# Transposing scaled queries and keys as fp16 halves by DMA instead of by TensorE, with every engine's order rearranged

## The chip, the cores and the metric

The kernel runs on one core of a Trainium2 chip. Its metric is the device time of one launch in microseconds. The core has five engines that run side by side, each through its own list of instructions in order, and wait for each other on semaphores: TensorE (PE: matrix products; PEld is its weight load), VectorE (DVE), ScalarE (ACT), GpSimd (POOL) and SyncE (SP, which here issues the DMAs). TensorE writes to PSUM, eight banks of 2 KB a partition; SBUF is the working memory.

## The reference, cut to what matters

A decoder layer on `x` of 32 batches of 112 tokens by 256, with 375 context rows a batch. Three blocks, each on a layer norm of `x` and each added to it:

```python
# attention, H = 8 heads of D = 128, M = 256
q, k, v = x @ wq, x @ wk, x @ wv           # per head, 112 x 128
q, k = rope(rmsnorm(q)), rope(rmsnorm(k))  # rmsnorm and rotation over the 128
s = (q * mult) @ (k * mult).T              # mult = (1/128) ** 0.5, causal mask
x = x + softmax(s) @ v @ wo
# context
h = layernorm(x) @ ctx.T                   # 112 x 375
x = x + gelu(h) @ ctx
# quantised feed-forward, 256 -> 1024 -> 256
x = x + linear_q(relu_q(linear_q(layernorm(x), w1, b1)), w2, b2)
```

## The kernel before

**Stages.** The loop is a software pipeline over batches, unrolled by four. In turn i each engine works on batch a = i (normalised input, the three projections, rotation and scaling of queries and keys), b = i-1 (scores, softmax, product with the values, output projection), c = i-2 (second layer norm, context block, quantised hidden layer) and, on TensorE and VectorE, d = i-3 (output layer). `FIRST`, `SECOND` and `THIRD` are the turns -1, 0 and 1 with orders of their own. Each engine's `body(i)` is an order written out by hand; every step waits for semaphores that count batches (`done(j)`) or half batches (`half(j, n)`).

**Precision.** Most products are made of three: high times high, high times low, low times high (`split_products`, `project`). A tile in high and low halves is made by a copy to the shorter type on ScalarE and a subtraction on VectorE.

**Queries and keys.** TensorE's `project(w, a, ...)` makes 12 products of 112x512. ScalarE squares the result from PSUM (`square_qk`), VectorE rotates it (`turn_cos`, `turn_sin`, `turn`) and sums the squares a head (`sum_squares`), GpSimd makes the inverse root (`rms_root`). The result is scaled by it into `qkn` (fp32): the queries on ScalarE, eight activations in two groups (`normalise_q`), the keys on VectorE, one instruction (`normalise_k`, L510). In the next turn TensorE transposes sixteen blocks of 112x128 into PSUM (`transpose_qk`, L888), ScalarE copies them to fp16 (`qkT_hi`) and VectorE subtracts to get `qkT_lo` (L557). Then come the scores.

**PSUM.** Banks are shared, so a writer must wait for the last reader of what lay there. The one that the argument turns on:

```python
q_ps, k_ps, v_ps = psum[0:T, 4:6, :], psum[0:T, 2:4, :], psum[0:T, 0:2, :]   # L194
f_ps = psum[:, 4:6, 0:FC // 2 * T]                                           # L203
pe.wait_ge(f_int_done, half(a.plus(-3), 1))                                  # L996, before project(0, a)
```

`f_ps` is the hidden layer of batch c, which ScalarE's `hidden(c)` reads at the end of its turn (eight activations, L788); `q_ps` is where the next turn's query projection goes.

**DMAs.** SP stores the output rows of d, loads the context of batch c+2 twice (rows, 375 KB, once ScalarE and GpSimd have split the last; columns, 375 KB, once they are used) and `x` of batch b+4 once its slot is free.

## Time and profile before

| | us |
|---|---|
| median of 3 runs (lowest to highest) | 731.12 (730.54 to 731.15) |
| the profiled execution | 730.84 |
| its span, first to last instruction | 728.8 |
| TensorE busy in it | 694.8 (95%) |
| VectorE busy | 654.9 (90%) |
| ScalarE busy | 518.7 (71%) |
| GpSimd busy | 308.5 (42%) |
| hardware DMA queue, share of 16 engines | 17.5% |

The profile is of one execution. Busy times are unions of an engine's instructions; an instruction's own duration is longer than the step to the next queued one, as neighbours overlap. The granted clock of TensorE was full in all but the first and the last slices of the page (0.985 over the span).

### The profile page before, as it was taken

The page shows a single profiled execution, that of the slowest core. Times are in us where ns is not written, and L with a number is a line of the kernel's source. Part 1 is how long each engine was busy: PE and PEld are TensorE (multiplying, and loading weights), DVE is VectorE, ACT ScalarE, POOL GpSimd, SP SyncE. Part 2 cuts the span into 40 slices and gives each one's busy share as a digit, 9 for nine tenths or more (in the row PEclk, how much of TensorE's full clock was granted, in tenths as well). Part 3 has the DMA queues.
Part 4 walks back from the last instruction along what each step waited for, and adds up shares of the span by engine and source line. Part 5 has one row for each costly group of instructions (what it writes and reads, how often), then busy time and mean ns, then how long its engine had stood idle before and what let it go on. Part 6 is the DMA issues. An engine that isn't in the chain of part 4 may idle for free.

```text
span 728.8 us, 15471 instructions
## 1 busy us (share of the span) xinstructions
PE 694.8 (95%) x5600; PEld 611.3 (84%) x5600; DVE 654.9 (90%) x1264; ACT 518.7 (71%) x1290; POOL 308.5 (42%) x425
## 2 busy tenths in 40 slices
PE   5599999999999999999999999999999999999974
PEld 4478888898888989898898989889888988988863
DVE  5989999999999999999999999999999999999942
ACT  5657666777766677776667877666777766777742
POOL 1344434534444443444444344444434444543421
PEclk9799999999999999999999999999999999999996
DMA  7601111011111101111110111111011111101100
GB/s 255 217 7 49 51 57 53 25 49 49 48 55 55 51 22 49 48 48 55 55 47 24 51 48 48 55 55 46 23 52 49 48 55 56 48 18 48 44 7 13
DMA packets 23946, 38.86 MB, mean 53 GB/s; under 512 B 2048, under 2 KB 18896, under 8 KB 23664
## 3 DMA queue, kind: packets, MB, share of 16 engines
q1 hardware_dynamic: 23920, 38.51, 17.5%
q8 instruction: 16, 0.26, 0.2%
q14 instruction: 10, 0.08, 0.0%
HBM read 34.84 MB, written 3.67 MB: 53 GB/s over the span
## 4 chain that ended last, share of the span: by engine, by line
PE 87%; DVE 5%; ACT 3%; issue 2%; DMA 1%; POOL 1%; SPq 0%; POOLq 0%; DVEq 0%; ACTq 0%
PE psum L880 34%; PE psum L867 22%; PE psum L908 7%; PE psum L888 7%; PE psum L945 5%; PE psum L978 4%; PE psum L970 3%; PE psum L915 3%; PE psum L936 2%; DMA w_raw<-in_wv 1%; DVE turn_c L489 1%; DVE ss L481 1%; DVE turn_s L498 1%; POOL rms L357 1%; ACT w_raw L764 1%
## 5 line engine op out<-in xcount | busy, mean ns | idle before, releaser
L880 PE MATMUL psum<-wqkv_hi,xnT_hi 128*112 128x512 f32 x384 | 159.7, 416 | 4.8 <-DVE wqkv_lo L446 2.7
L880 PE MATMUL psum<-wqkv_lo,xnT_hi 128*112 128x512 f32 x384 | 152.5, 397 | 0.0
L880 PE MATMUL psum<-wqkv_hi,xnT_lo 128*112 128x512 f32 x384 | 131.8, 397 | 0.0
L350 POOL TENSOR_TENSOR rstd<-ve,nhalf 112x1 f32<-112x1 f32 x96 | 55.5, 578 | 142.7 <-DVE ve L420 137.7
L357 POOL TENSOR_TENSOR rms<-ms,nhalf 112x8 f32<-112x8 f32 x64 | 106.3, 1662 | 5.0
L718 ACT ACTIVATE sq<-psum 112x1024 f32<-112x1024 f32 x64 | 65.0, 1015 | 59.4 <-PE psum L880 59.4
L764 ACT ACTIVATE w_raw<-psum,rden 112x128 f32<-112x128 f32 x256 | 69.6, 384 | 45.4 <-DVE rden L532 45.4
L361 POOL TENSOR_TENSOR ctx_lo<-ctx_in,ctx_hi 125x768 fp32r<-125x768 f32 x32 | 58.6, 1830 | 92.5 <-ACT ctx_hi L691 92.5
L880 PEld LDWEIGHTS psum<-wqkv_hi,xnT_lo 128*112 128x112 f32 x384 | 67.7, 176 | 22.3
L880 PEld LDWEIGHTS psum<-wqkv_hi,xnT_hi 128*112 128x112 f32 x384 | 68.1, 177 | 20.4 <-issue 3.1
L774 ACT ACTIVATE qkn<-turn_c,rms 112x128 f32<-112x128 f32 x256 | 83.1, 427 | 1.1 <-POOL rms L357 1.1
L481 DVE TENSOR_REDUCE ss<-sq 112x4 f32<-112x512 f32 (+1 forms) x95 | 81.9, 862 | 0.0
L880 PEld LDWEIGHTS psum<-wqkv_lo,xnT_hi 128*112 128x112 f32 x384 | 68.3, 178 | 15.0
L489 DVE TENSOR_TENSOR turn_c<-psum,cos_t 112x1024 f32<-112x1024 f32 x64 | 77.9, 1217 | 1.4 <-ACT sq L718 1.4
L867 PE MATMUL psum<-wo_hi,oT_hi 128*112 128x256 f32 x256 | 78.2, 306 | 0.7 <-DVE oT_lo L564 0.7
L505 DVE TENSOR_TENSOR turn_c<-turn_c,turn_s 112x1024 f32<-112x1024 f32 x64 | 77.9, 1217 | 0.1
L498 DVE TENSOR_TENSOR turn_s<-psum,sin_t 112x1024 f32<-112x1024 f32 x64 | 77.4, 1210 | 0.0
L867 PE MATMUL psum<-wo_hi,oT_lo 128*112 128x256 f32 x256 | 71.8, 280 | 0.0
L867 PE MATMUL psum<-wo_lo,oT_hi 128*112 128x256 f32 x256 | 71.5, 279 | 0.0
L557 DVE TENSOR_TENSOR qkT_lo<-psum,qkT_hi 128x896 f16<-128x896 f32 x64 | 69.4, 1086 | 0.1
L788 ACT ACTIVATE f_int<-psum,b_col 128x112 int16<-128x112 f32 x256 | 66.6, 399 | 1.8 <-PE psum L970 1.8
L908 PEld LDWEIGHTS psum<-v_sb,w_raw 112*112 112x112 f32 x512 | 60.8, 176 | 3.6
(90 smaller groups left out, 1725.9 us busy)
## 6 DMA issues: line engine op xcount, KB each, us to landing
ctx_in<-in_ctx_rows SPq DMA_DIRECT2D x32, 375.0 KB
ctxT<-in_ctx_cols SPq DMA_DIRECT2D x32, 375.0 KB, 6.4
x_in<-in_x SPq DMA_DIRECT2D x32, 112.0 KB, 2.0
out_y<-y_out SPq DMA_DIRECT2D x32, 112.0 KB, 1.9
w_raw<-in_w SPq DMA_DIRECT2D x2, 1024.0 KB, 6.5
w_raw<-in_wq SPq DMA_DIRECT2D x2, 512.0 KB, 4.6
w_raw<-in_wk SPq DMA_DIRECT2D x2, 512.0 KB, 6.6
w_raw<-in_wv SPq DMA_DIRECT2D x2, 512.0 KB, 8.5
```

The source lines that it names most:

```text
L357: pool.tensor_tensor(rms[:, w, :], ms[:, w, :], nhalf[:, 0:H], ALU.pow).then_inc(qk_rms_done[w], 1)
L481: return dve.tensor_reduce(ss[:, w, hs], heads(sq[:, w, :])[:, hs, :], AX_X, ALU.add)
L489: dve.tensor_tensor(turn_c[:, w, :].rearrange("t (b h d) -> t b h d", b=2, d=D), (q_ps, k_ps)[w].rearrange("t b (h d) -> t b h d", d=D), c ...
L498: dve.tensor_tensor(turn_s[:, w, :].rearrange("t (h two f) -> t h two f", two=2, f=HALF), halves, table, ALU.mult).then_inc(sin_done[w], 1)
L505: dve.tensor_tensor(turn_c[:, w, :], turn_c[:, w, :], turn_s[:, w, :], ALU.add).then_inc(qk_turned[w], 1)
L557: dve.tensor_tensor(qkT_lo[:, w, :].rearrange("p (b n) -> p b n", b=2), (qT_ps, kT_ps)[w], qkT_hi[:, w, :].rearrange("p (b n) -> p b n", b=2),
L764: last = act.activation(on[:, h * D:(h + 1) * D], o_ps[:, h // OH, (h % OH) * VW:(h % OH) * VW + D], ACT.Copy, scale=rden[:, h:h + 1])
L774: last = act.activation(qkn[:, 0, h * D:(h + 1) * D], turn_c[:, 0, h * D:(h + 1) * D], ACT.Copy, scale=rms[:, 0, h:h + 1])
L788: last = act.activation(f_int[:, c * T:(c + 1) * T], f_ps[:, c // (FC // 2), (c % (FC // 2)) * T:(c % (FC // 2) + 1) * T], ACT.Relu, bias= ...
L867: product = pe.matmul(dst, lh, rh, start=first and k == 0, stop=last and k == len(terms) - 1)
L880: last = pe.matmul(ps[:, n, :], left[:, c, :], right[:, c, w, n * BANK:(n + 1) * BANK], start=c == 0 and left is xnT_hi and right is wqkv_ ...
L908: last = pe.matmul(o_ps[:, h // OH, at:at + VW], p_sb[:, h * T:(h + 1) * T], v_sb[:, h, :], start=h % OH == 0, stop=h % OH == OH - 1 or h ...
```

## The change

Queries and keys are now treated alike. ScalarE scales the rotated rows into fp16 (`normalise_qk`, eight activations each), VectorE subtracts that from the scaled row in eight instructions each (`split_qk`), and both halves lie in token layout in `qk16`. SP then issues one DMA transpose each for queries and keys, 112 x 2048 fp16 (448 KB) from SBUF to SBUF, straight into the layout of the scores. TensorE's transposes and the copies and subtractions after them go. The output layer's PSUM tile moves from bank 7 to bank 3. SP's loop is written out for all batches instead of looping. The orders of the engines are rearranged; the diff has them all.

```diff
+        qk16 = sb("qk16", [T, 2, 2, HD], F16)
+        qkT = sb("qkT", [P, 2, 2 * H, T], F16)
-        f2_ps = bank(7, M)[0:T]
+        f2_ps = bank(3, M)[0:T]
...
 SP
+            def transpose_qk(w, j):
+                sp.wait_ge(qk_lo_done[w], done(j))
+                sp.dma_start_transpose(qkT[:, w], qk16[:, w].rearrange("t l n -> t (l n)")).then_inc(
+                    qkT_landed[w][j.off % SLOTS], 16)
...
                     load_ctxT(nxt)
                 nxt = b.plus(SLOTS)
+                if a.inside(B):
+                    if b.inside(B):
+                        sp.wait_ge(s_ready, done(b))
+                    transpose_qk(0, a)
+                    transpose_qk(1, a)
                 if b.inside(B) and nxt.inside(B):
                     sp.wait_ge(x2_done, done(b))
                     load_x(nxt)
-            iterations(sp, body)
+            for n in range(-1, B + 3):
+                body(Batch(0, n))
...
 GpSimd
                 if C:
                     split_ctx(c)
+                if A:
+                    rms_root(0, a)
                 if B_ and A:
                     mask_later_keys(b)
-                if A:
-                    rms_root(0, a)
...
 VectorE
+            def split_qk(w, j):
+                dve.wait_ge(qk_hi_done[w], done(j))
+                for h in range(H):
+                    at = slice(h * D, (h + 1) * D)
+                    last = dve.scalar_tensor_tensor(out=qk16[:, w, 1, at], in0=turn_c[:, w, at], scalar=rms[:, w, h:h + 1],
+                                                    in1=qk16[:, w, 0, at], op0=ALU.mult, op1=ALU.subtract)
+                last.then_inc(qk_lo_done[w], 1)
...
 ScalarE
-            def normalise_q(n, j):
+            def normalise_qk(w, n, j):
                 if n == 0:
-                    act.wait_ge(q_turned, done(j))
-                    act.wait_ge(q_rms_done, done(j))
+                    act.wait_ge(qk_turned[w], done(j))
+                    act.wait_ge(qk_rms_done[w], done(j))
+                    if j.has(1):
+                        act.wait_ge(qkT_landed[w][(j.off - 1) % SLOTS], landed(j.plus(-1)))
                 for h in range(n * HH, (n + 1) * HH):
-                    last = act.activation(qkn[:, 0, h * D:(h + 1) * D], turn_c[:, 0, h * D:(h + 1) * D],
-                                          ACT.Copy, scale=rms[:, 0, h:h + 1])
+                    last = act.activation(qk16[:, w, 0, h * D:(h + 1) * D], turn_c[:, w, h * D:(h + 1) * D],
+                                          ACT.Copy, scale=rms[:, w, h:h + 1])
                 if n == 1:
-                    last.then_inc(q_normed, 1)
+                    last.then_inc(qk_hi_done[w], 1)
```

The orders of one steady turn, before and after (a, b, c, d as above; n is the batch after a):

```
TensorE before: transpose_qk(0), (1) b | project q a | out_units d | xn2 rows c | scores b | ctx_hidden c
                project k a | weigh_values b | ctx_out c | project v first half a | transpose_o(0) b
                project v second half a | transpose_o(1) b | xn1 rows n | project_out b, 4 heads, with
                transpose_xq c after two | hidden_units c | project_out b, last 4 heads
TensorE after:  project q a | out_units d | xn2 rows c | ctx_hidden c | project k a | scores b | ctx_out c
                project v first half a | weigh_values b | project v second half a | transpose_o(0), (1) b
                then as before
VectorE before: split_qkT(0) b | normalise_x2 c | split_qkT(1) b | residual_out d | turn_cos, turn_sin(0) a
                sum_squares(0) a | gelu_inner c | normalise_x n | gelu_outer c | turn(0) a | split_g c
                turn_cos(1) a | invert_sums b | turn_sin(1) a | residual_ctx c | sum_squares(1) half a
                split_oT(0) b | quantise_x3 c | sum_squares(1) half a | split_oT(1) b | turn(1) a
                split_xnT n | normalise_k a | residual_attention b | stats | clip_hidden c
VectorE after:  normalise_x2 c | residual_out d | turn_cos, turn_sin(0) a | gelu_inner c | sum_squares(0) a
                gelu_outer c | turn(0) a | split_g c | normalise_x n | turn_cos, turn_sin(1) a
                residual_ctx c | sum_squares(1) a | invert_sums b | split_qk(0) a | quantise_x3 c
                split_oT(0) b | turn(1) a | split_oT(1) b | split_xnT n | split_qk(1) a
                residual_attention b | stats | clip_hidden c
ScalarE before: split_qkT(0), (1) b | square_qk(0) a | copy_xn2T, split_ctx c | softmax_exp b
                square_h, tanh_h, split_g c | square_qk(1) a | normalise_o(0), (1) b | split_oT(0) b
                copy_v(0), normalise_q(0) a | split_oT(1) b | split_xnT n | copy_xqT c
                copy_v(1), normalise_q(1) a | hidden c
ScalarE after:  split_ctx c | square_qk(0) a | copy_xn2T, square_h, tanh_h, split_g c | square_qk(1) a
                softmax_exp b | normalise_qk(0), both groups a | normalise_o(0), (1) b | copy_v(0) a
                split_oT(0) b | copy_v(1) a | split_oT(1) b | split_xnT n | copy_xqT c
                normalise_qk(1), both groups a | hidden c
```

## Rows read from the trace of the kernel before

**Rows 1.** The page, first section: busy time, share of the span, instructions.
```profile
PE 694.8 (95%) x5600; PEld 611.3 (84%) x5600; DVE 654.9 (90%) x1264; ACT 518.7 (71%) x1290; POOL 308.5 (42%) x425
```

**Rows 2.** Windows, one steady turn: length, busy of each engine, clock, DMA.
```profile
326.20:347.50 21.30, 21.30 (x177) 18.88 (x176) 20.03 (x40) 15.78 (x42) 9.58 (x13) 1.00 0.16 47
```

**Rows 3.** Chain of waits, one steady turn: start us, us, what.
```profile
304.88 1.68 PE psum L888 x16
306.56 2.80 PE psum L880 x12
...
315.78 1.77 PE psum L908 x16
```

**Rows 4.** Chain of waits, batch 2's projection and the tail.
```profile
50.99 2.81 PE psum L880 x12
...
668.70 2.80 PE psum L880 x12
...
692.45 1.42 PE psum L867 x24
...
700.02 2.17 ACT w_raw L764 x8
```

**Rows 5.** Timeline of ScalarE, same turn: start us, us, instruction, idle before it.
```profile
337.25 1.01 ACT L718 ACTIVATE sq<-psum 112x1024 f32<-112x1024 f32 x1
339.70 2.17 ACT L764 ACTIVATE w_raw<-psum,rden 112x128 f32<-112x128 f32 x8 [1.45 <-DVE rden L532]
341.76 0.55 ACT L691 ACTIVATE oT_hi<-psum 128x448 fp32r<-128x448 f32 x1
...
345.29 1.27 ACT L774 ACTIVATE qkn<-turn_c,rms 112x128 f32<-112x128 f32 x4
346.46 2.05 ACT L788 ACTIVATE f_int<-psum,b_col 128x112 int16<-128x112 f32 x8
```

**Rows 6.** Groups by line and shape: busy us, mean ns, idle before.
```profile
L557 DVE TENSOR_TENSOR qkT_lo<-psum,qkT_hi 128x896 f16<-128x896 f32 x64 | 69.4, 1086 | 0.1
```

**Rows 7.** Timeline of VectorE, same turn.
```profile
331.55 0.42 DVE L584 SCALAR_TENSOR_TENSOR y_out<-psum,x3b 112x256 f32<-112x256 f32 x1 [0.67 <-PE psum L978]
331.89 1.21 DVE L489 TENSOR_TENSOR turn_c<-psum,cos_t 112x1024 f32<-112x1024 f32 x1
...
336.32 0.50 DVE L522 SCALAR_TENSOR_TENSOR g<-h_t,psum 125x336 f32<-125x336 f32 x1 [0.23 <-ACT h_t L738]
...
339.43 0.23 DVE L532 RECIPROCAL rden<-psum 112x6 f32<-112x6 f32 x2
...
342.50 0.61 DVE L564 TENSOR_TENSOR oT_lo<-psum,oT_hi 128x448 fp32r<-128x448 f32 x1
343.03 0.41 DVE L550 TENSOR_SCALAR xq_int<-x,mv,rstd 112x256 int16<-112x256 f32 x1
...
343.61 0.68 DVE L481 TENSOR_REDUCE ss<-sq 112x4 f32<-112x512 f32 x1
344.42 0.63 DVE L564 TENSOR_TENSOR oT_lo<-psum,oT_hi 128x448 fp32r<-128x448 f32 x1
344.96 1.21 DVE L505 TENSOR_TENSOR turn_c<-turn_c,turn_s 112x1024 f32<-112x1024 f32 x1
...
346.40 1.68 DVE L510 TENSOR_TENSOR qkn<-turn_c,rms 112x1024 f32<-112x1024 f32 x1
```

**Rows 8.** Timeline of TensorE, a projection that starts after a stall.
```profile
21.61 0.49 PE L880 MATMUL psum<-wqkv_hi,xnT_hi 128*112 128x512 f32 x1 [2.04 <-DVE xnT_lo L439]
...
24.03 0.63 PE L880 MATMUL psum<-wqkv_hi,xnT_lo 128*112 128x512 f32 x2
```

**Rows 9.** DMA issues: tile, queue, count, KB each, median us to landing.
```profile
ctxT<-in_ctx_cols SPq DMA_DIRECT2D x32, 375.0 KB, 6.4
x_in<-in_x SPq DMA_DIRECT2D x32, 112.0 KB, 2.0
```

**Rows 10.** Windows in the tail.
```profile
690.00:695.00 5.00, 2.70 (x34) 2.27 (x34) 2.95 (x6) 2.02 (x4) 0.97 (x3) 1.00 0.08 23
```

More of the change, by code:

```diff
@@ L672, in body @@
                 if A:
-                    normalise_k(a)
+                    split_qk(1, a)
                 if B_:
@@ L850, in body @@
                 if A:
-                    copy_v(1, a)
-                    normalise_q(1, a)
+                    normalise_qk(1, 0, a)
+                    normalise_qk(1, 1, a)
                 if C:
@@ L883, in project, with scores @@
                     last.then_inc(ready, 1)
[L885 to L886 removed]
+            def scores(j):
+                pe.wait_ge(qT_landed[j.off % SLOTS], landed(j))
+                pe.wait_ge(kT_landed[j.off % SLOTS], landed(j))
                 for h in range(H):
[L888 to L897 removed]
                     last = split_products(s_ps[:, h // HH, (h % HH) * T:(h % HH + 1) * T],
[L899 removed]
+                                          [((qkT[:, 1, h, :], qkT[:, 1, H + h, :]), (qkT[:, 0, h, :], qkT[:, 0, H + h, :]))])
                 last.then_inc(s_ready, 1)
@@ L997, in body @@
                     project(0, a, q_ps, q_ready)
-                if i is THIRD:
-                    pe.wait_ge(v_copied, half(b, 1))
-                    transpose_qk(0, b)
-                    pe.wait_ge(k_sin_done, done(b))
-                    transpose_qk(1, b)
                 if D_:
                     out_units(d)
-                if B_ and not A:
-                    scores(b)
                 if C:
@@ L1010, in body @@
                     transpose_rows(xn2T_ps, xn2, xn2T_ready)
-                if B_ and A:
-                    scores(b)
-                if C:
-                    if c.has(1):
-                        pe.wait_ge(out_done, done(c.plus(-1)))
                     ctx_hidden(c)
+                if D_:
+                    pe.wait_ge(out_done, done(d))
+                if i is THIRD:
+                    pe.wait_ge(k_sin_done, done(b))
                 if A:
@@ L1019, in body @@
                 if B_:
-                    if A:
-                        pe.wait_ge(q_sin_done, done(a))
-                    weigh_values(b)
+                    pe.wait_ge(v_copied, half(b, 1))
+                    scores(b)
                 if C:
```

131 lines of the change are left out of this document (50 added, 81 removed).

## The prediction

> **What bounds the kernel now.** I read the page's first section first: TensorE is busy 95% of the span, VectorE 90% [rows 1], so either may be the bound. A window over one steady turn of the loop settles it: of 21.30 us TensorE is busy all, VectorE 20.03, ScalarE 15.78, GpSimd 9.58 [rows 2]. The chain of waits there consists of TensorE alone, block behind block: the sixteen transposes of queries and keys take 1.68 us of it, a whole projection 2.80, the value product 1.77 [rows 3]. In that chain the query projection of batch 2 starts at 50.99 and that of batch 31 at 668.70 [rows 4]: 29 turns of 21.30 us, with 51.0 us ahead of them and 60.1 behind.
>
> So 1.68 us of TensorE's work goes, which leaves 19.6 a turn. Whether that is gained depends on who is next. ScalarE's eight hidden-layer activations start at 346.46 and take 2.05, so they end at 348.51 [rows 5]. The transposes of 304.88 come round at 347.5 and end at 349.2 (two turns after [rows 3]), and then the next query projection runs, which overwrites the PSUM banks that the activations read (the wait on f_int_done in TensorE's body). The transposes cover 1.0 us of that wait; the slack behind it is some 0.6. If only the transposes went, TensorE would stand still for 1.0 of the 1.68 us. So that wait is what I follow in the new order.
>
> **The change part by part.**
>
> *TensorE*: minus 1.68 us a turn [rows 3]; everything else is moved, nothing added.
>
> *VectorE* loses two subtractions of 896 columns (1.086 each [rows 6], 1.00 start to start) and the key scaling (1.68, 1.61 start to start). It gains sixteen scalar_tensor_tensor of 112x128, which the trace doesn't show. Its queued ops step by their length at 0.96 elements a ns plus 0.065: 448 elements took 0.53 (342.50 to 343.03) [rows 7]. So 128 take 0.20 and sixteen 3.2. Ends: 0.17 if half the fixed part goes, 0.29 if nothing overlaps (the 0.42 of a 256-wide op at 331.55 less 128 elements). I take 0.20, as every queued row overlaps its neighbour. VectorE goes from 20.0 to 19.6 us, between 19.1 and 21.0.
> The Trainium skill ("VectorE: DVE Perf Modes", Side-by-side: where the cycles go) puts some 158 cycles ahead of an instruction's elements. By that a half costs 0.30 us, sixteen 4.8, and VectorE has 21.1 us a turn. The rows speak against it for queued instructions: the 448-wide one would step by 0.63, and it steps by 0.53.
>
> *ScalarE* loses two copies (0.86 each start to start, an estimate: 896 columns against 448 in 0.44) and gains eight key scalings, of which four take 1.17 (345.29 to 346.46) [rows 5]: 2.34. It goes to 16.4 us. The sum is no danger; the place is. The key scalings stand directly ahead of the hidden-layer activations, and wait for turn(1), which VectorE does after split_oT(0).
>
> *The loop this closes.* I walked all queues in their new order with start-to-start steps from these rows and 0.04 us for a semaphore. The same walk of the old order gives 21.32 us a turn, with waits of VectorE of 0.8 us before residual_out (0.67 at 331.55) and 0.3 before gelu_outer (0.23 at 336.32) [rows 7]. The new order, from the start of a query projection:
> - A projection that starts after a stall takes 3.0 us to its end (21.61 to 24.66 [rows 8]), 0.2 more than one behind other work. out_units 0.87, then residual_out 0.34 on VectorE: turn_cos(0) starts at 4.3; ScalarE's squares (1.01 [rows 5]) are done by then.
> - From turn_cos(0) to turn(1) VectorE took 344.96 - 331.89 = 13.07 us [rows 7]. Out go the idle 0.23 before gelu_outer, the second split_oT (0.54) and the 0.21 idle before it (343.61 + 0.60 to 344.42), and 0.07 for one reduction in place of two: 12.0. In comes split_qk(0), 1.6: 13.6. The last of it are invert_sums (0.15 start to start), split_qk(0), quantise_x3 (0.58) and split_oT(0) (0.53).
> - invert_sums so ends at 15.2. ScalarE scales the heads (2.06, 339.70 to 341.76), copies half of the values (0.48) and makes oT_hi (0.55) [rows 5]: 18.4. VectorE is at split_oT(0) at 17.3 and waits 1.1 for it.
> - split_oT(0) 0.53, turn(1) 1.21: 20.2. Key scalings 2.34, hidden-layer activations 2.05, semaphores: 24.6. Only then may the next query projection start.
>
> Unrounded the walk gives 24.32 and with the 0.2 of the restart 24.55, which I take. TensorE has 19.6 us of work and stands still for 4.7.
>
> *The landing*: split_qk(1) ends 24.3 us after the turn's start, and the scores are due 8.7 into the next turn. So each transfer may take 8.7 us from SP's queue to landing, hidden by the query projection, out_units, ctx_hidden and the key projection. A transfer of 448 KB within SBUF is in no row. Nearest: 112 KB landed in 2.0 us and 375 KB in 6.4, at whose rate 448 KB take 7.6 [rows 9]. Ends 2 and, if it moves in small pieces at half that rate, 15. I take 4 to 8, hidden. SP's new waits (scores, low halves; both behind the context loads) hold back the load of x, three batches ahead, and the next store, whose buffer is wanted four turns on: nothing.
> The Trainium skill ("DMA: Bandwidth & Descriptors", Latency and other measured facts) has 261 GB/s for a DMA transpose with a strided middle dimension. By that 458,752 bytes move in 1.8 us and the first rival below drops out. No trace here shows a transpose by DMA.
>
> *GpSimd*: same instructions; the mask now follows the queries' root, and still ends before the value product is due. Nothing.
>
> *Head and tail.* At the head ScalarE does eight key scalings (2.34) where it copied the transposed keys (0.97), ahead of the output weights, which VectorE awaits: plus 1.4, so 52.4. At the tail the last scores began 23.75 us after the last query projection (692.45 - 668.70) [rows 4]; now 24.3 + 0.4 + 4, plus 5.0. Against that the context product no longer runs behind them: the heads were scaled at 700.02 [rows 4], 7.6 after the scores began, and without it some 5.3 (scores, exponential, mask, value product). Net plus 2.7: 62.8.
>
> **Sum.** 52.4 + 29 x 24.55 (712.0) + 62.8 = 827.2 us of span. The profiled execution took 730.84 for a span of 728.8, so 2.0 lie around it: 829. It is 0.3 under the median of the runs shown, 731.12, which is nothing here.
>
> **Rivals.**
> 1. *The keys land late.* If a transfer takes L over 8.7 us, the loop is the landing, then scores to value product (5.5), invert_sums to oT_hi (3.3), split_oT(0), turn(1), scalings (4.2), split_qk(1) 1.6 and some 0.4 of semaphores and issue: L + 15. At L = 12 it is 27 a turn, 900 us; at 15, 987. For it: 7.6 us by the context's rate. Against it: nothing leaves the chip, and little else moves then.
> 2. *The halves are dear on VectorE.* Up to 0.33 each they hide in the 1.1 us wait. At 0.4 the walk gives 25.4 a turn, 853 us; at 0.5, 27.0, 900. Against it: no 256-wide row is over 0.43.
> 3. *Faster: TensorE stays the bound.* The one mechanism: the loop over f_int_done is shorter than TensorE's own 19.6 us, which then decides, and the run takes 731 - 30 x 1.68 = 681. Up to 21.3 the loop would still leave a gain. For it: VectorE and ScalarE each have less work than TensorE. Against it: with every stall left out the loop's rows still sum to 3.0 + 1.1 + 13.6 + 1.2 + 2.34 + 2.05 + 0.1 = 23.4. I would have to be 2 us off on a path of measured steps.
> 4. *TensorE's clock falls in the gaps.* In the tail it was granted 1.00 with TensorE busy 2.70 of 5 us [rows 10]; here it would be busy 19.6 of 24.5. At the lower of its two levels throughout, TensorE alone would need 39 us a turn, some 1,250 in all.
>
> **How the numbers follow.** Forecast 69%: 829, its own range 795 (23.4 a turn, no stall at split_oT) to 858 (25.5, if VectorE's new steps beside GpSimd stretch as the key scaling did: 1.68 where an addition of that length took 1.21 [rows 7]). Late landing 13%, dear halves 5%, clock 4%, faster 7%, and 2% for a loop that ends at the old time. A measurement of this kernel can tell about 0.2% from no change. Slower 0.91, same 0.02, faster 0.07. The range 788 to 875 leaves out the faster case, the clock and most late landings.
>
> **What would show it.** Right: in a steady turn TensorE idles 4 to 5 us, the largest piece (1.7) right before the query projection, the others before transpose_o and project_out; ScalarE goes from key scalings into the activations without a gap; VectorE waits about 1.1 us for oT_hi and 1.7 for the keys' high halves. Wrong: scores released by a DMA (rival 1), a mean of the halves over 0.33 (rival 2), TensorE without gaps (rival 3), a granted clock under 1 in the steady part (rival 4), or a turn under 23.4 us.

## The result and the profile after

| | before | after |
|---|---|---|
| median us (lowest to highest, runs) | 730.83 (730.49 to 731.15, 4) | 869.21 (868.35 to 874.89, 4) |
| profiled execution, span | 730.84, 728.8 | 869.32, 867.4 |
| mean granted clock of TensorE | 0.985 | 0.946 |

The changed kernel takes 1.1906 times as long (95% interval 1.1874 to 1.1938). It was forecast slower, at 829; it is 40 us slower than that. It lies inside the range of 788 to 875, but above 858, where the prediction had the upper end for its own mechanism: that the range holds it is in part luck.

The page's first section, to be read against [rows 1]. TensorE lost its 512 transposes but not its busy time, since a matmul counts longer where the engine restarts or runs at half clock (one of 512 columns 0.48 and 0.63 us, queued at full clock 0.40); VectorE got 38 us more.

```profile
PE 716.8 (83%) x5088; PEld 585.0 (67%) x5088; DVE 693.2 (80%) x1649; ACT 548.7 (63%) x1482; POOL 361.8 (42%) x425
```

Windows of 25 us, about one turn each, with the columns of [rows 2]. No engine is full now. TensorE stands still for 3.65 us of the first window, less than the 4 to 5 that the prediction gave as its sign. In the second its clock is under 1.

```profile
322.00:347.00 25.00, 21.35 (x161) 17.44 (x160) 21.24 (x52) 16.71 (x46) 11.39 (x15) 1.00 0.34 77
347.00:372.00 25.00, 21.28 (x150) 16.98 (x148) 19.58 (x50) 15.86 (x46) 9.73 (x13) 0.93 0.33 73
```

The chain of waits over one steady turn, from query projection to query projection: 25.02 us (forecast 24.55). In [rows 3] it was TensorE alone. Now it goes from TensorE to VectorE (314.62 to 325.6), to ScalarE (heads, 325.63), through `split_oT` (328.76) and the output projection (329.44) to `copy_xqT` (330.55), the key scalings (L775), the hidden layer's activations (L789), and back: the loop that the prediction walked, save for the two steps at 329.44 and 330.55.

```profile
310.21 3.05 PE psum L881 x12
313.26 0.89 PE psum L971 x8
...
314.62 1.22 DVE turn_c L501
...
325.63 0.06 ACT w_raw L763
...
328.30 0.44 ACT oT_hi L695
...
328.76 0.64 DVE oT_lo L573
...
329.44 0.96 PE psum L868 x6
...
330.55 0.04 ACT xqT L695
...
333.24 1.95 ACT f_int L789 x8
...
335.23 3.04 PE psum L881 x12
```

The view of waits (who waited for whom: us in total, times, longest). The first two are the new standstills of VectorE and TensorE. The last is the only one of TensorE for a transfer of queries or keys, and it is in the head.

```profile
DVE qk L524 <- ACT qk L775: 64.2, 32, 2.7
PE psum L881 <- ACT f_int L789: 42.7, 29, 1.8
...
PE psum L868 <- DMA qkT<-qk: 7.4, 1, 7.4
```

The timeline of VectorE in that turn, against [rows 7]. The eight halves at 325.51 are followed 2.09 us later, so they step by 0.26; `xq` takes 0.64; and VectorE reaches `split_oT` at 328.7, just when oT_hi is there.

```profile
325.51 2.17 DVE L524 SCALAR_TENSOR_TENSOR qk<-turn_c,rms,qk 112x128 f16<-112x128 f32 x8
327.60 0.41 DVE L565 TENSOR_SCALAR xq_int<-x,mv,rstd 112x256 int16<-112x256 f32 x1
328.04 0.64 DVE L418 TENSOR_SCALAR xq<-xq_int 112x256 bf16<-112x256 int16 x1
328.76 0.62 DVE L573 TENSOR_TENSOR oT_lo<-psum,oT_hi 128x448 fp32r<-128x448 f32 x1
```

The DMA issues, against [rows 9]: a transpose of 448 KB lands 4.0 us after its issue. The context's columns land in 5.8 us (6.4 before), `x_in` in 2.9 (2.0).

```profile
qkT<-qk SPq DMA_TRANSPOSE x64, 4.0
```

TensorE's timeline (first two lines) and a 5-us window. After a standstill of 1.82 us the query projection begins with matmuls that step by 0.23 to 0.30 us, as everywhere; from 361.0 on they step by 0.43. The granted clock of the window is 0.66: TensorE runs at the lower of its two levels (1.2 instead of 2.4 GHz) for 3.4 us, then is back.

```profile
360.27 0.46 PE L881 MATMUL psum<-wqkv_hi,xnT_hi 128*112 128x512 f32 x1 [1.82 <-ACT f_int L789]
...
363.12 0.63 PE L881 MATMUL psum<-wqkv_hi,xnT_hi 128*112 128x512 f32 x1
```
```profile
360.00:365.00 5.00, 4.73 (x16) 3.50 (x16) 2.46 (x12) 0.98 (x3) 3.07 (x5) 0.66 0.58 115
```

In such windows from 90 to 785 us there are 37 us at half clock in all, eleven stretches; a turn with one takes 25.3 to 26.6 us. The kernel before has none from 90 to 660.

**Where the 40 us are.** The landmark is the square of a batch's queries on ScalarE, which starts as their projection ends: batch 2's at 59.19, batch 3's at 85.86, batch 31's at 794.41. The forecast puts 3.0 us between a projection's start and its square.

| part | forecast | measured | more |
|---|---|---|---|
| start to square of batch 2 | 52.4 + 3.0 = 55.4 | 59.2 | 3.8 |
| 29 turns | 712.0 | 794.41 - 59.19 = 735.2 | 23.2 |
| square of batch 31 to the end | 62.8 - 3.0 = 59.8 | 867.4 - 794.41 = 73.0 | 13.2 |

The tail's chain, against [rows 4]. The exponential (L727) stands behind `split_g` on ScalarE, GpSimd's mask (L385) behind the exponential, GpSimd's low half of the context (L373) behind the mask, and the context product (828.55) behind that; the value product (L901) is queued behind it on TensorE. The heads are scaled (L763) at 833.57, which is 42.2 us after the last query projection began (794.41 - 3.0); before it was 31.3, the forecast says 34.0. The value product takes 2.48 us here and 1.93 in a batch before; the granted clock is 0.72 from 820 to 840 and 0.63 from 840 to 867, where [rows 10] showed 1.00. From the heads to the end it is 33.8 us (867.4 - 833.57), and before it was 28.8 (728.8 - 700.02): 5.0 more, of which some 3.5 are steps that run through TensorE's matmuls at half clock, and 1.5 a scaling on VectorE that takes 1.88 us beside GpSimd (see the last section). So 8.2 of the 13.2 us that the forecast missed lie ahead of the heads and 5.0 behind them.

```profile
824.64 0.81 ACT w_raw L727
...
825.71 0.93 POOL w_raw L385
826.64 1.78 POOL ctx_lo L373
...
828.55 2.23 PE psum L868 x9
830.79 2.48 PE psum L901 x16
...
833.57 2.18 ACT w_raw L763 x8
```

### The profile page after: what moved, and what is told of

It reads as the page before. It is cut to its first block, busy times and chain, and to the rows that moved or that the text cites. A ratio compares the mean times of both kernels' runs of the same rounds, so it can differ in the third digit from the quotient of the medians.

```text
span 867.4 us, 14896 instructions
## 1 busy us (share of the span) xinstructions
PE 716.8 (83%) x5088; PEld 585.0 (67%) x5088; DVE 693.2 (80%) x1649; ACT 548.7 (63%) x1482; POOL 361.8 (42%) x425
## 2 busy tenths in 40 slices
DMA packets 140684, 68.23 MB, mean 79 GB/s; under 512 B 118784, under 2 KB 135632, under 8 KB 140400
## 3 DMA queue, kind: packets, MB, share of 16 engines
q1 hardware_dynamic: 140656, 67.88, 33.8%
## 4 chain that ended last, share of the span: by engine, by line
DVE 42%; ACT 26%; PE 21%; issue 8%; DMA 1%; POOL 1%; SPq 1%; ACTq 0%; POOLq 0%; DVEq 0%
PE psum L881 11%; ACT qk L775 8%; DVE turn_c L501 8%; DVE turn_s L510 8%; ACT w_raw L763 7%; ACT f_int L789 6%; DVE ss L493 6%; PE psum L868 5%; DVE turn_c L517 4%; PE psum L971 3%; DVE oT_lo L573 2%; ACT v_sb L695 2%; DVE h_t L531 2%; DVE g L537 2%; DVE stat L423 2%
## 5 line engine op out<-in xcount | busy, mean ns | idle before, releaser
L881 PE MATMUL psum<-wqkv_hi,xnT_hi 128*112 128x512 f32 x384 | 162.7, 424 | 49.0 <-ACT f_int L789 42.7
L524 DVE SCALAR_TENSOR_TENSOR qk<-turn_c,rms,qk 112x128 f16<-112x128 f32 x512 | 139.7, 346 | 64.2 <-ACT qk L775 64.2
L775 ACT ACTIVATE qk<-turn_c,rms 112x128 f16<-112x128 f32 x512 | 156.4, 389 | 27.2 <-POOL rms L369 25.9
L369 POOL TENSOR_TENSOR rms<-ms,nhalf 112x8 f32<-112x8 f32 x64 | 150.6, 2353 | 5.0
L360 POOL TENSOR_TENSOR ve<-mv,ln_eps 112x1 f32<-112x1 f32 x64 | 14.6, 228 | 298.7 <-DVE mv L428 298.7
L868 PE MATMUL psum<-wo_hi,oT_hi 128*112 128x256 f32 x256 | 83.9, 328 | 21.3 <-DVE oT_lo L573 21.2
L763 ACT ACTIVATE w_raw<-psum,rden 112x128 f32<-112x128 f32 x256 | 69.7, 384 | 44.0 <-DVE rden L547 44.0
L510 DVE TENSOR_TENSOR turn_s<-psum,sin_t 112x1024 f32<-112x1024 f32 x64 | 77.8, 1216 | 0.0
L493 DVE TENSOR_REDUCE ss<-sq 112x8 f32<-112x1024 f32 x64 | 77.5, 1210 | 0.0
L868 PE MATMUL psum<-wo_hi,oT_lo 128*112 128x256 f32 x256 | 76.4, 298 | 0.0
L868 PE MATMUL psum<-wo_lo,oT_hi 128*112 128x256 f32 x256 | 76.1, 297 | 0.0
L367 POOL TENSOR_TENSOR ms<-ss,rms_eps 112x8 f32<-112x8 f32 x64 | 18.5, 288 | 129.1 <-DVE ss L493 129.1
L901 PEld LDWEIGHTS psum<-v_sb,w_raw 112*112 112x112 f32 x512 | 60.8, 182 | 14.4 <-issue 14.4
```

The costliest lines, as they stand in the source:

```text
L369: pool.tensor_tensor(rms[:, w, :], ms[:, w, :], nhalf[:, 0:H], ALU.pow).then_inc(qk_rms_done[w], 1)
L493: return dve.tensor_reduce(ss[:, w, hs], heads(sq[:, w, :])[:, hs, :], AX_X, ALU.add)
L510: dve.tensor_tensor(turn_s[:, w, :].rearrange("t (h two f) -> t h two f", two=2, f=HALF), halves, table, ALU.mult).then_inc(sin_done[w], 1)
L524: last = dve.scalar_tensor_tensor(out=qk16[:, w, 1, at], in0=turn_c[:, w, at], scalar=rms[:, w, h:h + 1], in1=qk16[:, w, 0, at], op0=ALU.m ...
L763: last = act.activation(on[:, h * D:(h + 1) * D], o_ps[:, h // OH, (h % OH) * VW:(h % OH) * VW + D], ACT.Copy, scale=rden[:, h:h + 1])
L775: last = act.activation(qk16[:, w, 0, h * D:(h + 1) * D], turn_c[:, w, h * D:(h + 1) * D], ACT.Copy, scale=rms[:, w, h:h + 1])
```

## Experiments

All are variants of the changed kernel, unless said otherwise. Each median stands beside the kernel before on the same chip (731.37, 730.26, 730.43 and 731.26 in the four sets).

### Is the bank shared with the hidden layer what holds the query projection?

`e1_banks` puts the hidden layer's sums into banks 2 and 3, so that the key projection waits for its activations in place of the query projection.

```diff
-        f_ps = psum[:, 4:6, 0:FC // 2 * T]
+        f_ps = psum[:, 2:4, 0:FC // 2 * T]
@@ body of TensorE
-                        pe.wait_ge(f_int_done, half(a.plus(-3), 1))
                     project(0, a, q_ps, q_ready)
...
+                        pe.wait_ge(f_int_done, half(a.plus(-3), 1))
                     project(1, a, k_ps, k_ready)
@@ hidden_units and out_units wait for all readers of those banks
+                        pe.wait_ge(oT_lo_done, half(b, 1))
-                    if c % (FC // 2) == 0:
-                        pe.wait_ge(f_q_done, half(j, c // (FC // 2)))
+                pe.wait_ge(f_q_done, half(j, 1))
```

> The hidden layer's PSUM tile moves from banks 4 and 5 to banks 2 and 3, so that the query projection no longer waits for f_int; the wait stands before the key projection instead. Theory A (the loop from the key scalings over the hidden-layer activations to the query projection sets the turn): the query projection starts as soon as TensorE is there, and the same path comes back 0.8 us shorter a turn over out_units, which waits for the clipped hidden layer: some 24.2 us a turn against 25.0, about 845 us in all. Rival B (the keys' landing sets the turn) and rival C (VectorE's sixteen small instructions set it): the wait was slack, the time stays at 869.

Measured 846.78 us (845.89 to 847.67), ratio 1.1581 [1.1539, 1.1624]; an undisturbed turn is 24.2 us, and three stretches at half clock are left of eleven. The size came as expected, which is in part luck: the mean turn fell by 1.03 us (25.31 to 24.28), as stretches at half clock went too, and head and tail together are some 5 us longer here. The wait is real, and 0.8 us a turn lie behind it, not more: the next loop is close. It runs through the same key scalings, but on through VectorE. The chain of that kernel from them to the next `copy_xn2T`:

```profile
325.07 0.99 ACT qk L775 x3
326.08 0.36 DVE qk L524 x2
...
326.61 1.66 DVE qk L524 x6
...
329.80 0.28 DVE f_q L580
...
330.12 1.08 PE psum L970 x8
```

### Does the place of the key scalings matter?

`e9_hidfirst` turns the two around on ScalarE: first the activations, then the keys.

```diff
 @@ body of ScalarE
-                if A:
-                    normalise_qk(1, 0, a)
-                    normalise_qk(1, 1, a)
                 if C:
...
                     hidden(c)
+                if A:
+                    normalise_qk(1, 0, a)
+                    normalise_qk(1, 1, a)
```

> ScalarE's hidden-layer activations go ahead of the key scalings. If only the wait at the query projection counts, f_int is ready 2.4 us earlier and the turn falls to about 23.3 us, 820 in all. Theory A in full says that it gets worse: the key scalings end 2 us later, VectorE stands in split_qk(1) until then, and the clipping of the hidden layer, which is VectorE's last step, comes later, so that out_units right behind the query projection waits some 3 us for it. By the walk of the queues the turn is 2.0 us longer than now: 27.0, about 927 us.

Measured 988.19 us (987.01 to 989.37), ratio 1.3515 [1.3463, 1.3568]; turns of 28.2 to 29.5 us. Slower, as the walk of the queues says, and worse than it says. The wait that was avoided (query projection on `f_int`) is down to 0.5 us, and VectorE's for the keys' high halves is up to 5.1 (in the changed kernel 2.7):

```profile
DVE qk L524 <- ACT qk L775: 145.5, 32, 5.1
```

The miss of 61 us is in part the clock: 160 us of 810 are at half clock, one or two stretches in every turn. A change that looked like freeing TensorE lengthens the loop, since behind the keys on VectorE stand the statistics and `clip_hidden`, for which `out_units` waits.

### Was the stall at `split_oT` a term of its own?

`e3_copy` lets ScalarE make oT_hi before it copies half of the values (0.48 us earlier).

```diff
 @@ body of ScalarE
-                if A:
-                    copy_v(0, a)
                 if B_:
                     split_oT(0, b)
                 if A:
+                    copy_v(0, a)
                     copy_v(1, a)
```

> ScalarE copies the first half of the values after split_oT(0) instead of before it. Theory A: oT_hi is ready 0.48 us earlier, which VectorE waits for before turn(1), and all of it comes off the turn: 24.55 against 25.0, about 855 us. Rivals B and C: no change, 869.

Measured 865.01 us (863.18 to 866.83), ratio 1.1831 [1.1763, 1.1898]; an undisturbed turn is 24.85. Of the 0.48 us, 0.15 come through. oT_hi is there at 530.93 in the turn looked at, but VectorE gets to `split_oT` only at 531.34, busy with its halves (2.2 us) and with `quantise_x3` (0.82 and 0.23 in this turn). The 1.1 us of stall that the forecast had there were no stall but VectorE's work.

### Are the halves dear, or the bound?

`e2_whole` makes the low halves by one subtraction of 1024 columns. It leaves the root mean square out of the low halves.

```diff
-                for h in range(H):
-                    at = slice(h * D, (h + 1) * D)
-                    last = dve.scalar_tensor_tensor(out=qk16[:, w, 1, at], in0=turn_c[:, w, at], scalar=rms[:, w, h:h + 1],
-                                                    in1=qk16[:, w, 0, at], op0=ALU.mult, op1=ALU.subtract)
+                last = dve.tensor_tensor(qk16[:, w, 1, :], turn_c[:, w, :], qk16[:, w, 0, :], ALU.subtract)
```

> VectorE makes each low half with one subtraction over 1024 columns instead of eight scalar_tensor_tensor; the scale by the root is left out of the low halves, and only of them. VectorE has 2.0 us less work a turn. Theory A: before split_oT(0) VectorE only waits longer for oT_hi, and the second split is off the path, so the turn stays at 25.0, about 869 us, at most 0.2 us a turn less. Rival C (VectorE's small instructions set the turn): 2.0 us a turn less, about 811 us.

Measured 869.29 us (866.86 to 871.73), ratio 1.1889 [1.1804, 1.1974]; undisturbed turns as in the changed kernel. VectorE has 74 us less to do in all (busy 619.4), one instruction of 1.21 us in place of eight in 2.2, and the time stays. What it wins before `split_oT` it loses there, waiting for oT_hi (1.46 us in this line of its timeline):

```profile
327.37 0.62 DVE L570 TENSOR_TENSOR oT_lo<-psum,oT_hi 128x448 fp32r<-128x448 f32 x1 [1.46 <-ACT oT_hi L692]
```

So rival 2 is out: the halves cost a third more than I took, and it costs nothing. With `e3_copy` this shows the two paths into `split_oT(0)`, ScalarE's and VectorE's, to be within 0.15 us of each other; shortening one alone brings no more than that.

### Do the transfers hold anything?

`e4_extra1` puts one spare transpose of half the size ahead of the keys' and waits for it; `e5_extra3` three in a row.

```diff
                 sp.wait_ge(qk_lo_done[w], done(j))
+                if w == 1:
+                    sp.wait_ge(spare_set, 1)
+                    for n in range(1):   # 3 in e5_extra3
+                        sp.dma_start_transpose(spare[:, :, :], spare_in[:, :]).then_inc(spare_landed, 16)
+                        sp.wait_ge(spare_landed, 16 * (1 * (done(j) - 1) + n + 1))   # 3 * (done(j) - 1) in e5_extra3
                 sp.dma_start_transpose(qkT...
```

> SP transposes a spare tile of half the size by DMA and waits for its landing before it issues the keys' transpose, so that the keys land some 3 us later than now (7 us after the low halves are done, against 4.0). Theory A: the keys have 8.7 us, nothing changes, 869. Rival B (the landing is on the path): 3 us a turn more, about 956.

Measured 868.43 us (866.59 to 870.27), ratio 1.1887 [1.1846, 1.1929].

> The same with three spare transposes in a chain, so that the keys land some 9 us later, 13 us after the low halves. Now the slack of 8.7 is used up and the loop over the landing, L + 15, sets the turn: 28 us, about 956 in all. If the slack were much larger than I worked out, the time would stay at 869.

Measured 1011.11 us (1009.62 to 1012.59), ratio 1.384 [1.3799, 1.3882]. The DMA table and the waits of the latter:

```profile
spare<-spare_in SPq DMA_TRANSPOSE x96, 2.7
```
```profile
PE psum L877 <- DMA qkT<-qk: 118.0, 32, 15.7
```

One spare transfer, 2.7 us to landing, is hidden whole; three show, 3.3 us of wait a turn behind the head's 15.7. So in the changed kernel the keys have at least 2.7 us to spare, and rival 1 is a real mechanism that lies beyond this kernel's transfers. Its size here is 55 us over what was expected: turns of 26.7 to 32 us, mean 29.6, with 118 us at half clock.

### What would it bring to leave the transposes out, with nothing put in their place?

`e6_notr` is the kernel before with four of its sixteen transposes a batch. It leaves the other heads' blocks of transposed queries and keys unwritten (zeros at first).

```diff
                 pe.wait_ge(qk_normed[w], done(j))
-                for h in range(H):
+                for h in range(0, H, HH):
```

> The kernel before, with two of eight transposes of queries and of keys each; the other heads' blocks are left out of the computation (PSUM is zeroed once at the start). TensorE has 1.2 us less work a turn. If TensorE alone set the turn, the time would fall by 30 x 1.2, to 695. By the slack that I read (0.6 us before the query projection meets f_int) most of it is lost to that wait: the walk gives 20.9 us a turn against 21.3, about 719.

Measured 721.83 us (720.86 to 724.42), ratio 0.9893 [0.9866, 0.9919]; a turn is 20.95 us against 21.30. Twelve transposes of 0.105 us (a sixteenth of 1.68 [rows 3]) are 1.26 us, and 0.35 come through. The prediction said that most of it would be lost in the wait on f_int_done. The size is right, the culprit is another one: that wait is 0.3 us long, and the chain comes from VectorE's key scaling (L510), which the few transposes that are left wait for:

```profile
321.07 1.69 DVE qkn L510
...
322.81 0.41 PE psum L889 x2
```

The kernel before is balanced in this sense: these twelve transposes are worth less than a third of their length to it, some 1%, and any new step on the other engines has to be paid for out of that. What it would bring to have none left that waits for the key scaling was not run.

### How much of the loss is the new order, and how much the halves and the DMA?

`e7_oldorder` has the DMA transposes and the halves, with the engines' orders of the kernel before: on VectorE both `split_qk` follow `turn(1)`, where the key scaling was; on ScalarE the key scalings follow the query scalings; GpSimd masks ahead of the queries' root; TensorE's body as before, without the transposes. The diff is against the kernel before.

```diff
 @@ body of VectorE, at the place of normalise_k
-                    normalise_k(a)
+                    split_qk(0, a)
+                    split_qk(1, a)
 @@ body of ScalarE
-                    normalise_q(1, a)
+                    normalise_qk(0, 1, a)
+                    normalise_qk(1, 0, a)
+                    normalise_qk(1, 1, a)
```

> The change's DMA transposes with the order of every engine as before it; split_qk(0) and split_qk(1) stand where normalise_k stood, the key scalings behind those of the queries, ahead of the hidden layer. If the new order is what the change needs to be worth anything, this is slower than 869. By the walk of the queues it is 1.1 us a turn faster than the new order: split_oT(0) no longer waits, and the loop is the same otherwise; 23.9 us a turn, about 837. In either case it is slower than before (731), as the loop over the key scalings and the hidden-layer activations is there too.

Measured 859.95 us (859.7 to 860.19), ratio 1.1771 [1.1742, 1.1801]. The old order is 1.1% faster than the new one, and slower than expected by 23 us. A steady turn takes 25.24 in the mean, and every one has one or two stretches at half clock, 130 us of 695. TensorE stands still for 3.4 us before the query projection, and this is what it then does (chain of that kernel):

```profile
306.89 1.94 ACT f_int L790 x8
...
308.87 5.46 PE psum L882 x12
314.33 1.27 PE psum L972 x8
```

At full clock these two took 3.04 and 0.89. So some 2.8 us of this turn's 26.1 are the clock's, and without them it is 23.3: near the expected 23.9 (this turn alone; an estimate). The loss is thus in what the change does, halves on the scaling path ahead of the activations, in either order. The 9 us that the old order is faster do not come from the steady turns, whose means are 25.24 and 25.31, but from the tail: from the square of batch 31 to the end it takes 64.1 us (858.0 - 793.87) where the changed kernel takes 73.0.

### Do the standstills bring the half clock?

`e8_fill` puts five idle matmuls of 512 columns ahead of the wait on f_int_done; `e12_fillall` seven there, three ahead of the transposes of the heads and three ahead of the output projection. No result of theirs is read.

```diff
                     if a.has(3):
+                        for _ in range(7):   # e8_fill: 5, with xnT_hi[:, 0, :] in place of the first wqkv_hi
+                            pe.matmul(psum[0:T, 7, :], wqkv_hi[:, 0, 0, 0:T], wqkv_hi[:, 0, 0, 0:BANK], start=True, stop=True)
                         pe.wait_ge(f_int_done, half(a.plus(-3), 1))
 @@ e12_fillall also ahead of transpose_o(0, b) and of project_out(range(0, HH // 2), b)
+                        for _ in range(3):
+                            pe.matmul(psum[0:T, 3, :], wqkv_hi[:, 0, 0, 0:T], wqkv_hi[:, 0, 0, 0:BANK], start=True, stop=True)
...
```

> The changed kernel with five matmuls of 512 columns into an unused bank right before TensorE waits for f_int; their result is used by nobody. They take 1.2 of the 1.7 us that TensorE stands still there. If the dips of TensorE's clock that the trace shows (stretches of 3.4 us at 0.5 in about every third turn) come from its standing still, they go, and with them the 0.3 us a turn by which the mean turn (25.3) exceeds the undisturbed one (25.0); the restart of the query projection saves up to 0.2 more: 24.8 a turn, about 855 us. If the dips have another cause, or cost nothing, the time stays at 869.

Measured 865.49 us (862.0 to 867.16), ratio 1.1834 [1.179, 1.1877]; 20 us at half clock in the steady part, where the changed kernel had 37. Fewer, not gone: 0.57 us of standstill were left ahead of the query projection, and the other two pauses were whole. Six stretches against eleven alone would say little: `e4_extra1` and `e11_tail`, with the pauses of the changed kernel, have nine each, `e2_whole` has thirteen.

> Thirteen idle matmuls of 512 columns a turn (into banks that are free there, results never read) stand in TensorE's pauses: seven ahead of the wait for the hidden layer's activations, three ahead of the transposes of the heads, three ahead of the output projection. Theory: the stretches at half clock come from TensorE's pauses, and go if all are filled: of the eleven in the steady part none is left, the granted clock there is 1.00, turns stay at 25.0 us, and the run takes some 859 us (29 turns times 0.35 less). Rival: they come from the power of the other engines or from TensorE's load itself: at least as many as before (eleven), 869 us or more.

Measured 862.63 us (860.08 to 863.43), ratio 1.1782 [1.1755, 1.1808]. A window of it: TensorE is busy 24.16 of 25 us, at 1.00.

```profile
322.00:347.00 25.00, 24.16 (x173) 19.55 (x174) 21.29 (x52) 16.70 (x47) 11.07 (x13) 1.00 0.34 77
```

No 5-us window from 90 to 785 us is under 1.00, all turns lie between 24.93 and 25.04, and their mean is 24.96 against 25.31. More work for TensorE, less time: the dips came from its pauses, and cost 0.35 us a turn. The run is 6.6 us faster than the changed kernel's median; I had expected 10. In the profiles the 28 turns give the 9.8 us, and head and tail are 4 us longer here (batch 3's square at 87.39 against 85.86, the tail 75.4 against 73.0).

### The tail

`e11_tail` lets GpSimd make the low half of the context ahead of the mask in the drain as well.

```diff
 @@ body of GpSimd
-                if B_ and not A:
-                    mask_later_keys(b)
                 if C:
                     split_ctx(c)
                 if A:
                     rms_root(0, a)
-                if B_ and A:
+                if B_:
                     mask_later_keys(b)
```

> GpSimd forms the low half of the context ahead of the mask in the drain too, as it does in a steady turn. Theory: the tail's excess hangs in part on GpSimd's order: the mask waits for the exponential at 825.5 and ctx_lo (1.8 us) behind it releases the context product at 828.55, ahead of which the value product can't run. With ctx_lo early, the context product starts when the low half of g is there (about 825.2) and the value product at about 827.3 in place of 830.8: 3.5 us less, 865.7 us. Rival: the exponential, behind split_g on ScalarE, sets it, and under 1 us is gained: 869 us.

Measured 868.14 us (867.55 to 870.78), ratio 1.1877 [1.1852, 1.1902], which doesn't tell it from the changed kernel. In its profile the tail (square of batch 31's queries to the end) is 865.9 - 794.99 = 70.9 us instead of 73.0, and the value product follows the mask directly:

```profile
819.78 1.89 DVE xn L485
...
828.25 0.81 ACT w_raw L725
...
829.31 0.94 POOL w_raw L385
...
830.30 2.04 PE psum L899 x16
```

From the end of the mask to the end of the value product it is 2.1 us instead of 6.6, but the mask ends 3.0 us later after that square. Of these, 1.3 are the context's hidden product, which ran at half clock (2.87 us, in the changed kernel 1.58), and 1.5 the edit's own doing: the low half of the context (GpSimd, 819.71 to 821.5) now runs beside VectorE's scaling L485, which takes 1.89 us instead of 0.42. So the wait for ctx_lo was real, and moving it up costs part of what it gives. The 2.1 us in all are within the spread of tails: `e8_fill` and `e12_fillall`, whose drain is the changed kernel's, have 73.1 and 75.4. The rest of the excess is read from the chain: the exponential behind the GELU steps on ScalarE, and the clock.

### The best that these parts give

`e10_halves` joins `e1_banks` and `e3_copy`, and ScalarE signals each group of four high halves, so that VectorE starts on the first four.

```diff
-                if n == 1:
-                    last.then_inc(qk_hi_done[w], 1)
+                last.then_inc(qk_hi_done[w], 1)
 @@ split_qk
-                dve.wait_ge(qk_hi_done[w], done(j))
                 for h in range(H):
+                    if h % HH == 0:
+                        dve.wait_ge(qk_hi_done[w], half(j, h // HH))
```

> Three repairs together: the hidden layer's tile in banks 2 and 3 (846 us alone), the first copy of the values behind split_oT(0) (865 alone), and ScalarE signals each group of four scaled heads, so that VectorE starts with the low halves 1.2 us earlier. Theory A: what is left of the loop runs over split_qk(1) and the clipping to out_units, and the halves take 1.1 us out of it: 22.7 us a turn by the walk of the queues, about 795. If VectorE's own work (20.6 us a turn with halves of 0.263 start to start) and not the chain of waits held the turn, little would come of it beyond the 24.2 of the banks alone.

Measured 808.09 us (806.2 to 813.06), ratio 1.1075 [1.1024, 1.1126]; undisturbed turns of 23.05 us, two stretches at half clock. 44% of the loss is back, and it is still 10.7% slower than the kernel before. VectorE's wait for high halves fell from 64.2 to 23.9 us. I expected 22.7 a turn and 795.

## Why the prediction was right, and where it was short

**Right: the direction and the loop.** The next query projection waits for the activations behind the key scalings, and these for what stands behind `split_oT(0)`. Landmarks from the projection's start, forecast and measured (310.21 onwards): `turn_cos(0)` 4.3 and 4.4; end of `invert_sums` 15.2 and 15.4; oT_hi 18.4 and 18.5; the wait of TensorE before the projection 1.7 and up to 1.8; that of VectorE for the high halves 1.7 and 1.9 to 2.0. `e1_banks` cut the loop where it was said to close, and the turn fell; `e9_hidfirst` closed it worse.

**Right: no transfer shows in a steady turn.** 4.0 us to landing, in the forecast's 4 to 8. `e4_extra1` showed at least 2.7 us of room, `e5_extra3` that the room has an end.
The Trainium skill's 261 GB/s ("DMA: Bandwidth & Descriptors", Latency and other measured facts) would make it 1.8 us, an estimate; from issue to landing this case measured more than twice that, with some 1.5 us of it SP's issue. By the skill's figure and by the trace alike, rival 1 drops out here.

**Mis-sized: the halves, 0.20 us.** They step by 0.26 (2.09 for eight; 346 ns mean in the group of 512), inside the bounds of 0.17 and 0.29. The choice by a plain tensor_tensor's fixed part was too low for one with a scalar pointer and three sources, but it cost nothing: `e2_whole`.
The Trainium skill ("VectorE: DVE Perf Modes", Side-by-side: where the cycles go) gives 0.30 for it, an estimate from its fixed cycles: 0.04 above the measured step, where my 0.20 is 0.06 below.

**Mis-sized: the stall of 1.1 us at `split_oT(0)`.** It is about 0.1. VectorE arrives at 18.5 where the walk had 17.3: 0.2 in the first part, 0.5 by the halves, 0.4 by `xq` (0.64 us beside GpSimd's addition, 0.24 in the tail).

**Mis-sized: the turn, 24.55.** It is 24.96 without dips. The step that failed is the last third of the walk. It had `turn(1)` release the key scalings; `copy_xqT` stands before them on ScalarE and waits for TensorE, which has to restart the output projection first (329.44 to 330.55). The scalings start at 330.80, some 0.25 us after `turn(1)` would have let them, and the first part of the walk took 0.1 to 0.15 more; scalings and activations took their 4.4. Over 29 turns the 0.4 us are 11.7. (A slip in the sum itself, 24.32 and 0.2 taken as 24.55, is 0.9 us in all.)

**Given as a rival, and it came in part: the clock.** "TensorE's clock falls in the gaps" stood at 4%, for a fall throughout. It fell in eleven stretches of 3.4 us. `e12_fillall` priced it: 28 turns times 0.35, 9.8 us. A granted clock under 1 in the steady part was a sign of being wrong by the prediction's own list. The step that failed is the reading of [rows 10]: a window in which TensorE is busy 2.70 of 5 us at 1.00 doesn't show that a steady loop with pauses of 1.8 us stays at 1.00. Another window of the kernel before, in its head, pointed the other way:

```profile
30.00:35.00 5.00, 2.00 (x19) 1.68 (x19) 4.21 (x11) 2.84 (x3) 0.89 (x2) 0.50 0.12 37
```

The third part of the turns' 23.2 us is 1.7, batch 2's own turn (26.67).

**Mis-sized: the head, plus 1.4.** It is 5.4 more than before (square of batch 2: 51.0 + 2.8 and 59.2). Three steps of it show in the trace. First, the scores of batch 0 wait for their transfer, with nothing beside them to hide it; they start at 35.39, before it was 33.54, though the last weights landed 1.3 us earlier in this run. The chain of the head:

```profile
26.20 2.11 DVE qk L524 x8
28.33 2.82 SPq L312
31.20 4.05 DMA qkT<-qk
```

I walked ScalarE in the head and left out the landing, though the prediction counted it (with 4 us) for the tail.

Second, GpSimd: the prediction put its new order at nothing, since the mask, behind the queries' root, "still ends before the value product is due". In the head it does not. The exponential ends at 38.81 and TensorE is through with half of the values' projection at 41.8, but the mask runs only at 44.01, behind the root and a small step of its own (L354) that takes 1.98 us here, beside VectorE's work, and 0.18 in a steady turn:

```profile
40.42 1.69 POOL L369 TENSOR_TENSOR rms<-ms,nhalf 112x8 f32<-112x8 f32 x1
42.07 1.98 POOL L354 TENSOR_TENSOR pool_cell<-pool_cell 1x1 f32<-1x1 f32 x1
44.01 0.98 POOL L385 TENSOR_SCALAR_AFFINE_SELECT w_raw<-w_raw 112x896 f32<-112x896 f32 x1
```
```profile
45.09 3.75 PE L901 MATMUL psum<-v_sb,w_raw 112*112 112x129 f32 x16 [3.33 <-issue]
```

That is 3.3 us of standstill before the value product. The kernel before had the mask ahead of the root, at 37.17, and no such pause; nor has `e7_oldorder`, with that order, and its square of batch 2 is at 55.50.

Third, the clock: the value product takes 3.75 us there and 1.93 before; the half clock lasts from 30.0 to 50.4, in the kernel before from 27.2 to 37.4. Together the three make the scaled heads 7.1 us late (49.16 against 42.04), and 1.7 of that are won back before batch 2's projection, where TensorE no longer has transposes.

In a steady turn the mask ends at 323.12 and the value product begins at 323.22, so there too GpSimd is only just in time.

**Mis-sized most, for its length: the tail, plus 2.7.** It is 15.7 more than before (from the square of batch 31: 728.8 - 668.70 - 2.80 = 57.3, and 73.0). The forecast counted that the context product no longer ran behind the last scores, and missed that its low half does stand between mask and value product (GpSimd's order in the drain), that the exponential is behind the GELU steps on ScalarE, and the clock. What it did count, 4 us for the landing, is not what held the scores: the keys' transfer was issued at 817.1 and landed some 4.0 later, and the scores began at 821.89, right behind the context's hidden product in TensorE's order. `e7_oldorder` shows the new order to be the larger part: with the old one the tail is 64.1, so some 9 of the 15.7 us hang on it (one profile each). `e11_tail` shows that the wait for ctx_lo is one step of that; how the rest divides between the exponential's place and the clock is read from the chain and not tested.

**Rivals 2 and 3.** Dear halves are out by `e2_whole`. TensorE is not the bound in the changed kernel (21.35 of 25.0), so the faster case is out too; `e6_notr` shows how little there was to win.

What stays open: whether a version with DMA transposes can beat the kernel before. VectorE's own work, with halves at 0.26, comes to some 20.6 us a turn by the walk, against 21.3 in the kernel before; `e10_halves` stands at 23.05. None tried got under.

## What to carry to other kernels

Where the engines are as close as here (21.30 and 20.03 us busy of a turn of 21.30), taking work off the busiest one is worth little (here 0.35 us of 1.26), and what is added elsewhere must be placed on the loop by name: walk every queue with start-to-start steps, and include the small copies (here `copy_xqT`) that an engine waits in front of the step in question. Walk head and tail with the same care: in the head a new transfer had nothing beside it, and an order that was just in time in the steady turn (root before mask) cost 3.3 us there. If the walk leaves TensorE with pauses, price the clock from a row that has such pauses in a steady loop, or test it by filling them.

## What the runs showed of the hardware

- TensorE's clock. With a standstill of 3.4 us before each query projection there were stretches at half clock in every turn (`e7_oldorder`), with 1.8 nine to thirteen in 28 turns (eleven in the changed kernel), with 0.6 and the other pauses left six (`e8_fill`), with all pauses filled none (`e12_fillall`).
- GpSimd beside VectorE. The root of the mean squares (L369) takes 1.65 us for the keys; for the queries it starts with a rotation sum of VectorE from two sources (343.83) and takes 3.11. In the kernel before, where that sum starts some 0.5 us behind it, it takes 1.65 for both. In the tail a scaling of 256 columns on VectorE (L487) takes 1.88 us from 845.64, beside GpSimd's subtraction for the context from 845.57; in the steady turn it takes 0.41. `e11_tail` moves that subtraction beside another scaling of the same shape, and this one goes from 0.42 to 1.89. The timeline of GpSimd, steady part:

```profile
343.87 3.11 POOL L369 TENSOR_TENSOR rms<-ms,nhalf 112x8 f32<-112x8 f32 x1
...
350.92 1.65 POOL L369 TENSOR_TENSOR rms<-ms,nhalf 112x8 f32<-112x8 f32 x1
```
- A DMA transpose within SBUF lands in 4.0 us for 448 KB and in 2.7 for 224 KB, counted from its issue, and SP is busy with the issue for 1.4 to 1.6 of them (once 2.8, the first). It moves in small pieces: 118,784 of the run's 140,684 packets are under 512 B, where the kernel before had 2,048 such of 23,946.
